# Five pairs in the load ring and four buffers for high parts, in place of six and three

## The reference, cut to what matters

```
# layer 0
u_comm = adj @ XB - sum(adj, axis=1) * XB
# layer 1
T1 = adj @ x;  T2 = 2*(adj @ T1) - x;  T3 = 2*(adj @ T2) - T1
# layer 2
h = (adj @ x + x) / (sum(adj, axis=1) + 1)
# layer 3
mask = adj != 0;  rank = cumsum(mask, axis=1);  w = mask * 0.5 ** (k - pos)   # pos from rank
out = w @ support + bias
```

## Time and profile before

| | |
|---|---|
| time, median of 3 runs | 3087.15 us (3086.23 to 3095.04) |
| the profiled execution's own time | 3095.84 us |
| its span | 3093.3 us |
| TensorE busy | 2952.4 us, 95% |
| VectorE busy | 2820.8 us, 91% |
| ScalarE busy | 2348.4 us, 76% |
| DMA engines busy | 94.6% on the queue of the loads |

### The profile page before, as it was taken

How to read it: one execution, slowest core, us unless ns; L and a number is a source line. 1 busy time by engine, 2 the same in 40 slices (tenths; PEclk the granted TensorE clock), 3 DMA queues, 4 the chain that set the end, 5 groups by cost and what they waited for, 6 DMA issues and landing times.

```text
span 3093.3 us, 35189 instructions
## 1 busy us (share of the span) xinstructions
PE 2952.4 (95%) x13425; PEld 2163.5 (70%) x13488; DVE 2820.8 (91%) x2397; ACT 2348.4 (76%) x1611; POOL 12.8 (0%) x30
## 2 busy tenths in 40 slices
PE   7999999999899999999989999988988999999998
PEld 5667677777688886888867888776766555555554
DVE  7999888888998889998899998999999999999997
ACT  5777776777777678777677767877777888888887
POOL 1000000000000000000000000000000000000000
PEclk9999999999999999999999999999999999999999
DMA  9999998998999999999999999989999999999996
GB/s 333 374 395 383 374 348 345 364 358 346 361 391 386 376 379 394 385 389 377 377 377 371 381 377 378 376 332 347 383 382 409 361 384 384 387 383 384 383 381 254
DMA packets 158982, 1148.09 MB, mean 371 GB/s; under 512 B 18145, under 2 KB 18321, under 8 KB 19553
## 3 DMA queue, kind: packets, MB, share of 16 engines
q1 hardware_dynamic: 157312, 1143.02, 94.6%
q0 software_dynamic: 1056, 2.41, 0.2%
q10 hardware_dynamic: 448, 0.43, 0.0%
HBM read 1143.69 MB, written 2.10 MB: 370 GB/s over the span
## 4 chain that ended last, share of the span: by engine, by line
PE 67%; DVE 23%; DMA 4%; ACT 3%; issue 3%; ACTq 0%; DVEq 0%
PE ACC L864 26%; DVE lo L609 17%; PE ACC L871 15%; PE ACC L979 14%; DMA raw<-in_at 4%; PE PST L993 4%; PE PSF L993 3%; ACT hi L432 2%; PE PST L887 1%; DVE SV L714 1%; PE PST L912 1%; PE PSF L936 1%; DVE M L624 1%; PE PSF L959 1%; PE PSF L939 1%
## 5 line engine op out<-in xcount | busy, mean ns | idle before, releaser
L609 DVE TENSOR_TENSOR lo<-raw,hi 128x2048 fp32r<-128x2048 f32 x832 | 1876.6, 2287 | 164.4 <-ACT hi L432 160.4
L432 ACT CAST hi<-raw 128x2048 fp32r<-128x2048 f32 x832 | 1584.0, 1912 | 546.8 <-PE ACC L864 339.6
L864 PE MATMUL ACC<-hi,T 128*128 128x512 f32 x4992 | 1284.9, 394 | 4.5 <-ACT hi L432 3.1
L864 PEld LDWEIGHTS ACC<-hi,T 128*128 128x128 f32 x4992 | 936.4, 189 | 218.1 <-issue 11.4
L871 PE MATMUL ACC<-lo,T 128*128 128x512 f32 x3200 | 889.1, 400 | 97.4 <-DVE lo L609 91.4
L871 PEld LDWEIGHTS ACC<-lo,T 128*128 128x128 f32 x3200 | 592.1, 190 | 290.8 <-DVE lo L609 174.8
L624 DVE SCALAR_TENSOR_TENSOR M<-raw,M 128x512 bf16<-128x512 f32 x1008 | 636.8, 686 | 41.1 <-PE ACC L979 24.3
L438 ACT ACTIVATE Wf<-ACC,w_bias 128x1024 fp32r<-128x1024 f32 x512 | 568.9, 1115 | 127.8 <-PE ACC L979 127.2
L979 PE MATMUL ACC<-M,rank_b 128*128 128x512 bf16 x1969 | 518.3, 382 | 12.2 <-ACT Wf L438 6.7
L979 PEld LDWEIGHTS ACC<-M,rank_b 128*128 128x128 bf16 x2032 | 158.9, 98 | 266.7 <-issue 132.2
L993 PE MATMUL PST<-Wf,S 128*128 128x512 f32 x512 | 209.1, 489 | 0.0
(11 more groups left out here) (149 smaller groups left out, 990.1 us busy)
## 6 DMA issues: line engine op xcount, KB each, us to landing
raw<-in_at SPq DMA_DIRECT2D x1088, 1024.0 KB, 6.8
SV<-in_x_cols SPq DMA_DIRECT2D x8, 256.0 KB, 12.8
out<-O POOLq DMA_DIRECT2D x7, 256.0 KB, 6.4
out<-O ACTq DMA_DIRECT2D x1, 256.0 KB, 2.0
bias<-in_bias_rows ACTq DMA_DIRECT2D x1, 128.0 KB, 11.1
l1w_sb<-in_l_w POOLq DMA_DIRECT2D x2, 64.0 KB, 8.2
rank_f<-in_rank_mats POOLq DMA_DIRECT2D x1, 128.0 KB, 9.6
w_sb<-in_w POOLq DMA_DIRECT2D x2, 64.0 KB, 10.7
```

What stands on the lines that cost most here:

```text
L432: nc.scalar.copy(hi[:, c % NH], raw[:, c % NR]).then_inc(hi_done, 1)
L609: tt(lo[:, c % NR], raw[:, c % NR], hi[:, c % NH].bitcast(f32), ALU.subtract).then_inc(lo_done, 1)
L864: ins = mm(acc[:, part], w, hi[:, p.c % NH, s, part], start=p.opens and s == 0 and i == 0, stop=False)
```

## The change

One of the six slots of the ring `raw` is given up, and its 8 KB per partition hold a fourth buffer of `hi`. Nothing else is changed: the slots are used as `c % NR` and `c % NH`, and the waits follow from the same two numbers, so the load of pair c now waits for pair c - 5, and the rounding of pair c for pair c - 4. The places of all steps stay.

```diff
--- before.py
+++ after.py
@@ -48,8 +48,8 @@
     G = N // P
     Q = BLK // P
     NP = 4
-    NR = 6
-    NH = 3
+    NR = 5
+    NH = 4
     NW = 4
     HALF = 512
     HID = w1.shape[1]
```

## The result

The changed kernel takes 3172.14 us (median of 4; 3168.19 to 3178.63) beside 3089.84 us of the kernel before in the same runs: a ratio of 1.0255, 95% interval 1.024 to 1.0269. It is slower by 2.5%, some 80 us. The forecast was slower by 16 us, 3103, in a range to 3124. The direction was right, the size five times too small. In experiments 4, 9 and 11 one execution each was over 1.5% above the fastest of its kernel, and the times given there leave it out.

What follows compares the result with a forecast made beforehand. It took TensorE, with 67% of the chain, as the main bound, loads and VectorE setting the pace in some stretches; 18.1 lost less 2.3 won gave 15.8 us, 3087.2 + 15.8 = 3103.0 us, range 3084 to 3124 (8 in 10).

Steps and rivals of the forecast that it cites:

- First and fifth part: Five slots in steady P groups (3.5 us spare) and counting stage: cost 0; start: 0 to 2.7 us, not added.
- a sign of being wrong: Longer P groups in sweeps 2 to 4 would show the prediction wrong; the 254 us stretch should keep its length.
- Second part: Fourth high buffer in steady P groups: ScalarE's 339.6 us of waiting costs nothing as TensorE is full; gain 0.
- Third part: Fourth high buffer elsewhere: the waits at c + 2 and c + 3 stop it; gain 2.3 us, bounds 0 to 16.3.
- The 2.3 us of the sum: One VectorE subtraction won once by the fourth high buffer outside the steady P groups, taken off the loss.
- Fourth part: Load-bound stretches: the sixth slot is one pair of store, lost once per stretch; 18.1 us, bounds 0 to 38.
- The fourteen pieces of the chain fall into ten stretches: Count of places where the slot is felt: five groups before 458 us, five single pieces after 2205 us.
- the 1.81 us by which a load is issued later: Price per load-bound stretch: a load waits one more freed slot, 1.81 us in an S group.
- That the later issue would be absorbed by the queue: Rival for the load-bound stretches: later issue only shortens the load queue; 3087 us, up to 9 either way, chance 0.30.
- the term would be 0: Load-bound stretches: by the page's fit two loads in flight keep the engines full, so five slots cost nothing.
- The fourth buffer as a gain: Rival: the fourth high buffer pays behind long TensorE steps in sweep 1's S groups; up to 16.3 us, 3071, chance 0.07.
- The rival with the larger loss, 3129: Fifth slot felt throughout sweep 5 (4 us) and the fourteen pieces cost the full 38 us; chance 0.13.

Runs made afterwards that it cites:

- experiment 4: Four slots and four high buffers, against the kernel before with six and three: 3361.44 us, ratio 1.093.
- experiment 9: Kernel before (six slots, three high buffers), but loads of sweep 1 only wait for pair c - 5: 3123.58 us, ratio 1.0092.
- experiment 11: Kernel before, but load c is issued only when load c - 2 has landed, at most two in flight: 3134.17 us, ratio 1.0117.
- experiment 5: Kernel before, but loads of the P groups of rows 4 to 7 in sweeps 2 to 4 wait for pair c - 5: 3099.43 us, ratio 1.0024.
- experiment 1: Five slots and three high buffers, the freed memory unused, against the kernel before: 3165.36 us, ratio 1.024.
- experiment 13: Half of each product-stage load left out, five slots and three high buffers, against the kernel before: 3098.95 us, ratio 1.0017.
- experiment 14: Half of each product-stage load left out, five slots and four high buffers, run once more against the kernel before: 3090.32 us, ratio 0.9987.
- experiment 6: Kernel before, but all product-stage loads except P groups of rows 4 to 7 in sweeps 2 to 4 wait for pair c - 5: 3167.11 us, 1.0243.
- experiment 8: Half of each product-stage load left out, five slots and four high buffers, against the kernel before: 3088.3 us, ratio 0.9982.
- experiment 2: Kernel before, but load c is issued only when load c - 3 has landed, at most three in flight: 3093.26 us, ratio 0.9998.

## Why the prediction was right in direction and wrong in size

**First and fifth part, the P groups and the counting stage: right for the steady groups, a little short in all.** In the stretch of the earlier trace rows the steady groups had 3.5 us to spare and lost nothing once their first row was over; TensorE stays at 254.98 of 256.5 us, and the 2.5 us belong to the groups D7 and P4 at its start. But the cost was not 0: by the ends of their last low matmuls all P groups of sweeps 2 to 4 together grew by 10 us, mostly P3 and P4, the first long ones behind D groups, and experiment 5 puts 7 us on the rows 4 to 7. I had named longer P groups as a sign of being wrong, and to this extent it came. The counting stage moved by some 2 us, twice what I allowed.

**Second part: right.** The wait for a high buffer was idle time on an engine that did not set the pace. It vanished (8.4 us are left of 339.6) and nothing came of it.

**Third part: right with full loads, and the reason too strong.** The fourth buffer won nothing in experiment 1 against the change. But the steps at c + 2 and c + 3 don't make it worthless: experiments 13 and 14 give 9 us. It is hidden in the change because no landed pair is left to be cast into it. The 2.3 us of the sum were not seen.

**Fourth part: the mechanism right, its term mis-sized, and this is nearly the whole error.** The sixth slot is one pair of store, and a stretch that eats its store loses it. The term was 10 x 1.81 = 18.1 us; the change cost 82, of which experiment 6 finds 75 outside the P groups of rows 4 to 7. Two factors failed.
The count failed most: "The fourteen pieces of the chain fall into ten stretches". The chain names only stretches in which loads already set the end. S5 was none of them, nor were S6, the D groups with the short P groups between them, or most of the rows of sweep 5; in all of these ScalarE waited for loads. In S5 the timeline shows what covered VectorE: one cast pair, less than the 2.5 us that were taken away; for the others that is argued from S5. The change put them on the chain: 52 pieces for fourteen. I had set aside the D groups since VectorE was busy for 96.63 of 97 us; that it was busy did not say by how much its loads came early. This stretch lost 6 us with VectorE's work unchanged. The second factor was the price: not the 1.81 us by which a load is issued later, but about the interval at which loads land in a row, 2.5 us. S3, S4 and S5 lost 2.6 to 2.8 us each, S6 1.8, but S1 and S2 lost 4.4 and 5.1, as if the store had been eaten twice. As an estimate, 82 us at 2.5 us each are 33 places in place of ten.
A better sign than the chain stands in the trace before: ScalarE waited for a load 205 times.

```profile
ACT hi L432 <- DMA raw<-in_at: 152.4, 205, 2.5
```

Each of these pairs has no landed pair behind it, and what covers it is only what the next engine holds. It is a sign and not yet a price: the five sweeps have 88, 22, 30, 17 and 48 such waits and lost 21.9, 7.6, 10.6, 9.6 and 30.5 us. Sweep 5, with such waits in more than half of its last 72 pairs (42), lost most, though sweep 1 has more of them. And waits alone cost nothing where the engine behind holds enough. Experiment 8, with five slots and short loads, has more than the kernel before and is no slower:

```profile
ACT hi L435 <- DMA raw<-in_at: 436.3, 498, 3.4
```

**The rivals.** That the later issue would be absorbed by the queue was wrong as a whole, but it was right of the fourth load in flight (experiment 2). The page "DMA: Bandwidth & Descriptors" of the Trainium skill, section Anatomy of one DMA, has the fit from which I estimated 4.4 us a load, by which two loads in flight carry the engines; a lone load took 4.7 to 4.8 us, near to it. That step holds while a load takes 4.9 us (sweep 5 of experiment 11) and not in the patches where it takes 6.5, which carry most of what the limit of two cost in its trace. The step from there to "the term would be 0" fails in either case: with six slots and two loads in flight sweep 5 took 410.8 us, with five slots and no such limit 432.4. The fourth buffer as a gain was worth 9 us without late loads, under its price of 16, and not in the change itself. The rival with the larger loss, 3129, was nearer in size than the forecast, but for another reason: landing times did fall, from 8.3 to 7.4 us (less than to the 6 that I gave), and the loss is not in sweep 5 alone.

The landing times of the changed kernel, operations on raw from 2239 to 2449 us, with ScalarE's waits for loads (32.0 us, 42 times before):

```profile
  DMA raw<-in_at: 59.8, 56
...
DMA to landing us min/median/max: 4.8/7.4/9.3
```

## What to carry to other kernels

When a slot is taken from a ring, don't count only the places where the chain already runs through a load. Look at every stretch in which the first reader of the ring waits for loads at all, and see how much the engine behind it holds in hand. Where that is less than one interval of the loads, one interval is the first estimate of the cost; here two of the S groups lost about two, and the rule was found after the result, no forecast has tried it. An engine that is 99% busy says nothing of how early its input comes: the slack must be read from the input's landing, pair by pair. Give slots to the ring whose emptiness stops the engine that sets the pace; idle time of the engine in front of it, 340 us here, is no reason.

## What the hardware showed that I had not expected

A 1 MB load took 4.7 to 4.8 us when nothing was queued, and loads in a row landed 2.5 us apart. From these two, two in flight should do, and for most of the span they did. But there are patches of 50 to 100 us in which a load takes 6.2 to 7.1 us even with only two in flight, and in them the kernel with the limit lost most of its time. Why is open. It was slower by 1.2% (0.5 to 1.8) and its times spread from 3105 to 3150 us, while the limit of three changed nothing (0.9998). And the ring's depth has a steep edge: from six to five slots 2.5%, from five to four another 6.8% of the time before (1.093 less 1.0255).
